# A GNN, token-mixing and routed FFN layer on one core: scattered chunks of four sorted records instead of two, batches of 28 columns instead of 30

## What is computed

```
xn = layernorm(x)
low  = relu(segment_sum(edge_weight    * (xn @ weight_low )[dst], src, N))
high = relu(segment_sum(edge_weight_n2 * (xn @ weight_high)[dst], src, N))
mlp  = relu(xn @ weight_mlp)
att  = softmax(sigmoid([low@a, high@b, mlp@c]) @ att_vec / 3)
gnn  = 3 * (att0*low + att1*high + att2*mlp)
mix  = linear attention of 8 heads over xn (K and V normalised), GELU MLP of 256, plus xn
x    = x + gnn + mix
w    = layernorm(x) @ wr + br
top  = the 3124 rows of largest w
x    = x + layernorm(x) + (top ? (gelu(layernorm(x) @ w1 + b1) @ w2 + b2) * w : 0)
```

## Time and profile before

| what | value |
|---|---|
| timed runs (3) | median 1985.35 us, 1983.74 to 1985.68 |
| profiled execution: span | 2481.7 us |
| mean granted TensorE clock in it | 0.835 |
| busy TensorE, VectorE, ScalarE, POOL | 1719.4, 1229.1, 924.8, 1371.7 us |
| indirect DMAs: scatters, gathers | 448, 852 |
| chain that ended last: TensorE, issue | 51%, 23% |

### The profile page before, as it was taken

How to read it: one execution, slowest core, us unless ns; L and a number is a source line. 1 busy time by engine, 2 the same in 40 slices (tenths; PEclk the granted TensorE clock), 3 DMA queues, 4 the chain that set the end, 5 groups by cost and what they waited for, 6 DMA issues and landing times.

```text
span 2481.7 us, 30518 instructions
## 1 busy us (share of the span) xinstructions
PE 1719.4 (69%) x9109; PEld 1441.9 (58%) x9109; DVE 1229.1 (50%) x3164; ACT 924.8 (37%) x2641; POOL 1371.7 (55%) x1351
## 2 busy tenths in 40 slices
PE   4788884998865347776777677677577677667672
PEld 4566673887754335665665666566466566556562
DVE  8899995888761223432343333333333333333336
ACT  2677873777652112321222222222222222222223
POOL 3277675788776565545555455455455545554600
PEclk9899996999967667888887888788788788788886
DMA  3221211111100422222222222222222222222303
GB/s 90 72 63 54 80 33 30 46 54 46 46 5 5 133 85 72 78 69 75 71 74 71 68 73 75 65 72 75 68 73 75 75 69 71 81 71 68 85 9 104
DMA packets 102212, 162.99 MB, mean 66 GB/s; under 512 B 32190, under 2 KB 72762, under 8 KB 102040
## 3 DMA queue, kind: packets, MB, share of 16 engines
q0 software_dynamic: 55232, 113.59, 16.4%
q1 hardware_dynamic: 46808, 47.29, 6.0%
HBM read 139.76 MB, written 21.04 MB: 65 GB/s over the span
## 4 chain that ended last, share of the span: by engine, by line
PE 51%; issue 23%; DVE 10%; ACT 9%; another core or an unknown queue 5%; DMA 1%; SPq 1%; POOL 0%; DVEq 0%; ACTq 0%; POOLq 0%
PE bank L1528 49%; ACT side L1303 2%; PE bank L1817 1%; ACT base L1303 1%; ACT arena L1303 1%; DVE arena L811 1%; ACT arena L1447 1%; ACT arena L1443 1%; DVE arena L733 1%; ACT side L1519 1%; DVE arena L766 1%; ACT arena L1307 0%; PE bank L1602 0%; DVE arena L781 0%
## 5 line engine op out<-in xcount | busy, mean ns | idle before, releaser
L1528 PE MATMUL bank<-arena 128*128 128x128 f32 (+3 forms) x6320 | 1292.5, 359 | 508.2 <-issue 426.8
L1528 PEld LDWEIGHTS bank<-arena 128*128 128x128 f32 (+1 forms) x6320 | 1094.8, 205 | 683.8 <-issue 500.0
L665 POOL DMA_INDIRECT arena<-xn_rows,arena x852 | 825.5, 969 | 733.8 <-SPq L564 450.0
L648 POOL DMA_INDIRECT sorted_records<-arena x448 | 523.0, 1167 | 256.0 <-issue 139.3
L1167 DVE CUSTOM_DVE_ANT_0 arena<-arena 128x256 f32<-128x256 f32 x98 | 37.8, 423 | 414.9 <-ACT arena L1452 376.1
L1122 DVE TENSOR_TENSOR arena<-arena 128x640 f32<-128x640 bf16 (+1 forms) x204 | 164.2, 805 | 47.6 <-DVE arena L1116 17.7
L1172 DVE SCALAR_TENSOR_TENSOR att_prod<-sg,att_neg 128x9 f32<-128x9 f32 x49 | 8.5, 174 | 334.9 <-issue 300.8
L1490 ACT ACTIVATE arena<-bank 128x256 f32<-128x256 f32 x49 | 18.8, 383 | 355.5 <-remote 262.1
L1116 DVE SCALAR_TENSOR_TENSOR arena<-io,arena 128x320 bf16<-128x320 f32 (+1 forms) x204 | 97.8, 479 | 106.3 <-DVE wall L1209 43.5
L1528 PE MATMUL bank<-arena,base 128*128 128x128 f32 (+3 forms) x766 | 118.4, 287 | 16.7 <-ACT base L1307 8.3
L1438 ACT ACTIVATE arena<-bank,b1f 128x128 f32<-128x128 f32 x392 | 110.3, 372 | 33.5 <-PE bank L1528 28.1
(11 more groups left out here) (312 smaller groups left out, 1889.2 us busy)
## 6 DMA issues: line engine op xcount, KB each, us to landing
arena<-xn_rows,arena POOLq DMA_INDIRECT x852
sorted_records<-arena POOLq DMA_INDIRECT x448
arena<-in_x SPq DMA_DIRECT2D x12, 512.0 KB
xn_rows<-arena SPq DMA_DIRECT2D x12, 512.0 KB
x_plus_xn_rows<-arena SPq DMA_DIRECT2D x12, 512.0 KB
arena<-x_plus_xn_rows SPq DMA_DIRECT2D x12, 512.0 KB
arena<-xn_rows SPq DMA_DIRECT2D x12, 512.0 KB
out<-base SPq DMA_DIRECT2D x4, 1024.0 KB
```

The source lines that it names most:

```text
L648: pool.indirect_dma_start(rec_dram, bass.IndirectOffsetOnAxis(ap=idx[0:PR, par, u:u + 1], axis=0), stage_rec[0:PR, par, u * 8:(u + 1) * 8] ...
L665: pool.indirect_dma_start(gring[:, c % GR, :], None, xn_dram, bass.IndirectOffsetOnAxis(ap=rring[:, c, 3:4].bitcast(I32), axis=0)).then_in ...
L1528: return pe.matmul(out_, lhsT, rhs, start=start, stop=stop, **kw)
```

## The change

A chunk is four records (64 bytes), `REC` = 4. A batch is 28 columns in two groups of 14, so there are 30 batches. A batch is scattered with 8 indirect DMAs and needs 8 small products for the chunks' places. Every bucket's run in a batch is padded to a multiple of four, so the bound on the columns becomes `COLS` = 900, in 8 blocks. All 13 mixing quads stand in slots 14 to 26 (`SPILL` = 0); slots 27 to 29 hold batches 27 to 29, and slot 30 the rest of the last. The first half's quotients are made in a batch's own slot and the second half's at the head of the next slot. The last bucket ends where its records end. The last tile's keys are masked by a memset and a copy of VectorE instead of a selection on POOL. Some small tiles lie elsewhere in memory.

```diff
-HG = 6
-BB = 30
-GS = 10
+HG = 7
+BB = 28
+GS = 14
+REC = 4
@@
-    UNITS = GC // 2
+    UNITS = GC // REC
     STEPS = PR * UNITS
-    CAP = 2 * STEPS
+    CAP = REC * STEPS
@@
-    COLS = 4 * -(-(E + NB * G) // (4 * P))
+    COLS = 4 * -(-(E + (REC - 1) * NB * G) // (4 * P))
@@
-    SPILL = 2
+    SPILL = 0
@@
-        quots = [base[:, spare:T * D].rearrange("p (j q) -> p j q", q=P), side[:, spare:T * D].rearrange("p (j q) -> p j q", q=P),
-                 r1.take([P, GS, P])]
+        quots = [r1.take([P, GS, P]) for _ in range(GROUPS)]
@@ scatter (POOL)
                     pool.indirect_dma_start(
                         rec_dram, bass.IndirectOffsetOnAxis(ap=idx[0:PR, par, u:u + 1], axis=0),
-                        stage_rec[0:PR, par, u * 8:(u + 1) * 8], None).then_inc(S(f"scattered{par}"), 16)
+                        stage_rec[0:PR, par, u * 4 * REC:(u + 1) * 4 * REC], None).then_inc(S(f"scattered{par}"), 16)
@@ end (POOL)
-            pool.wait_ge(S("w_ready"), T)
-            pool.affine_select(out=wkey[:, T - 1:T], in_=wall[:, T - 1:T], compare_op=ALU.is_ge, fill=SENTINEL,
-                               base=TAIL - 1, pattern=[[0, 1]], channel_multiplier=-1).then_inc(S("w_masked"), 1)
@@ sum_hots (VectorE)
-                    dve.tensor_tensor(many[:, :, 0:2], many[:, :, 0:2], many[:, :, 2:4], ALU.add).then_inc(S("many_set"), 1)
+                    dve.tensor_tensor(many[:, :, 0:3], many[:, :, 0:3], many[:, :, 4:7], ALU.add).then_inc(S("many_set"), 1)
...
-                    dve.tensor_tensor(many[:, :, 0], many[:, :, 0], many[:, :, 4], ALU.add).then_inc(S("many_set"), 1)
@@ counts (VectorE)
-            step(dve.tensor_scalar(cnt_b[0:NR, :], cnt_i[0:NR, :], 1, None, ALU.bitwise_and))
-            dve.tensor_tensor(runs[0:NR, :], cnt_i[0:NR, :], cnt_b[0:NR, :], ALU.add).then_inc(S("runs_ready"), 1)
+            step(dve.tensor_scalar(cnt_i[0:NR, :], cnt_i[0:NR, :], REC - 1, None, ALU.add))
+            step(dve.tensor_scalar(cnt_b[0:NR, :], cnt_i[0:NR, :], REC - 1, None, ALU.bitwise_and))
+            dve.tensor_tensor(runs[0:NR, :], cnt_i[0:NR, :], cnt_b[0:NR, :], ALU.subtract).then_inc(S("runs_ready"), 1)
@@ the buckets' table (VectorE)
-            step(dve.memset(pclip[:, NB:NR], float(COLS * P - 1)))
@@ slot (ScalarE)
                 if in_slot(g - 1):
-                    quotients(g - 1, 2, 1 - par)
+                    quotients(g - 1, 1, 1 - par)
...
-                if in_slot(g):
-                    quotients(g, 1, par)
                 if ln is not None:
                     ln_sqrt(ln)
@@ slot (TensorE)
                 if in_slot(g - 1):
                     permute(g - 1, 0, 1 - par)
-                    permute(g - 1, 1, 1 - par)
                 turn(0)
                 if in_slot(g - 1):
-                    permute(g - 1, 2, 1 - par)
+                    permute(g - 1, 1, 1 - par)
                 turn(1)
```

More of the change, by code:

```diff
@@ L283, in build @@
         ptab = lead_take("side", [1, NR], I32)
-        pcol = r1.take([1, NB + 1])
-        starts = r1.take([1, 2, NB])
-        span = r1.take([1, NB])
-        over = r1.take([1, NB])
-        over_sum = r1.take([1, NB])
-        words = r1.take([1, NB])
+        pcol = lead_take("side", [1, NB + 1])
+        starts = lead_take("side", [1, 2, NB])
+        span = lead_take("side", [1, NB])
+        over = lead_take("side", [1, NB])
+        over_sum = lead_take("side", [1, NB])
+        words = lead_take("side", [1, NB])
         far = r1.take([P, 2, NB])
@@ L775, in place @@
                 Q1 = 28
-                with nc.allow_low_precision(reason="whole numbers below 2 ** 13, one of a bucket's and at most nine ties"):
+                with nc.allow_low_precision(reason="whole numbers below 2 ** 13, one of a bucket's and at most thirteen ties"):
                     dve.tensor_tensor(prod[:, :, 0:H], prod[:, :, 0:H], prod[:, :, H:2 * H], ALU.add).then_inc(S("prod_half"), 1)
@@ L1225, in _ @@
             step(dve.memset(const_1_5[:, :], 1.5))
+            step(dve.memset(wkey[:, T - 1:T], SENTINEL))
             def end():
@@ L1416, in _ @@
             quotients(0, 0, 0)
+            ln_sqrt(0)
             quotients(0, 1, 0)
-            ln_sqrt(0)
-            quotients(0, 2, 0)
             stage_records(0, 0)
@@ L1544, in _ @@
             W = H2 * HG
-            PER = 10
+            PER = 8
             for g in range(G):
@@ L1747, in _ @@
             permute(0, 1, 0)
-            permute(0, 2, 0)
             schedule(pe, slot)
```

32 lines of the change are left out of this document (16 added, 16 removed).

## The result

| kernel | median | against the kernel before, same chip |
|---|---|---|
| before | 1983.78 us (5 runs, 1982.85 to 1985.68) | |
| after | 1968.86 us (5 runs, 1965.63 to 1971.53) | 0.992, 95% interval 0.9908 to 0.9932 |

The change makes the kernel 0.8% faster, 15 us, where 23 us slower were forecast. The profiled execution of the kernel after spans 1969.8 us with a mean granted clock of 0.933: no gaps of the kind of the earlier trace rows, so its rows are those of a timed run. That execution spans 1985.4 us at a clock of 0.926, and is free of the gaps too. All rows "of before" from here on are from it.

A forecast was written before the change was run, and what follows sets the result against it. The prediction took POOL as the bound, by scatters in front and then gathers. Front +4, gathers +25.4 and extra turns -6 sum to +23.4, so 1985.35 us becomes 2009 us, range 1964 to 2030.

The forecast's parts named there:

- POOL bounds both parts: Whole kernel before: POOL sets the pace, by scatters from batch 12 on, then by gathers at 1.27 us each.
- Scatters: Front: a batch's scatters cost POOL 24.5 us before and 12 after, so POOL leaves the path.
- A slot with LayerNorm, +0.3 us: Front, LayerNorm slots: the path is ScalarE's quotients and one permute; +0.3 us a slot, +4 over 12, bounds -13 and +13.
- A mixing slot, 22.35 + 1.0 = 23.35 us: Front, mixing slots: own pace 22.35 us; later quotients +1.7, longer permute +1.0, fewer small products -1.7.
- The lower clock: Rival, mixing slots: new idleness drops TensorE's clock; 24.5 us a slot gives 2024 us, 25.5 gives 2037; chance 0.15.
- The slots behind: Front, after the mixing slots: two batch-only slots of 17.5 us, then 28.1 us to the last index and 10.1 of scatters.
- Moving two quads: End of the front: moving mixing quads 11 and 12 ahead of the last batch earns nothing, at most 7 us.
- The 28 other gathers, the eighth block: Buckets: the 28 unneeded gathers run beside the kernel's end, the eighth record block under gathers; 0, block +1.7 without cover.
- Gathers, 20 x 1.27 = +25.4: Buckets: the last bucket needs 872 gathers instead of 852, each 1.27 us on POOL; +25.4 us.
- Extra turns, -6: Last bucket: eight extra turns of 1.9 us go, so it ends 2 us behind the last gather instead of 8; -6 us.
- the slots get faster: Rival, front: TensorE's work is the path, mixing slots take 21.2 us and LayerNorm slots 24.6; 1964 us, chance 0.18.
- the front's 0: Front, from slot 14's copy of ranks to the last scatter: 376.8 us after against 376.6 before, so nothing gained.

The follow-up runs named there:

- e3: The changed kernel with the last two mixing quads behind the batches again; 1970.62 us, 0.9919 of the kernel before.
- e4: The changed kernel with 872 columns instead of 900, leaving out the 28 gathers no bucket needs; 1968.07 us, 0.9898 of the kernel before.
- e2: The changed kernel with chunks of two records again and the last two mixing quads behind the batches; 2008.09 us, 1.0098 of the kernel before.
- e10: The kernel before with the last bucket ending where its records end, and small tiles moved as in the change; 1963.51 us, 0.9882.
- e8: The kernel before, unchanged, profiled again to get a profile without the TensorE gaps; 1987.09 us, span 1985.4 us.
- e5: The kernel before with chunks of four records in its old batches, 868 columns and the last bucket's true end; 1923.69 us, 0.9694.
- e6: The changed kernel with the second half's quotients made in the batch's own slot, in the 13 mixing slots only; 1946.85 us, 0.9815.
- e11: The changed kernel with its 8 small products made twice in each mixing slot; 1974.31 us, 0.9938 of the kernel before.

## Why the prediction was wrong

Its sum was +4 for the front, +25.4 for gathers, -6 for the last bucket. Measured are -20.2, +13.8 and -9.5. By its steps:

- **POOL bounds both parts**, the front from batch 12 on: right. Between 120 and 782 us its 432 scatters waited 46.9 us for places. One wait, ahead of the second batch, is 37.9; the others are seven of 1.0 us and one of 1.8, all ahead of slot 14. Up to there the slots go at VectorE's pace and POOL keeps up with them; behind it POOL has no wait for places at all.
- **Scatters**: 24.5 us for a batch before (24.3 in the mean of the clean profile), about 12 after (10.3 to 13.7 from a batch's first scatter to the end of its last), POOL no longer on the path in front: right.
- **A slot with LayerNorm, +0.3 us**: the first failure of the sum, 10.7 us. It took ScalarE's quotients and a permute for the path. The path is VectorE: before, it works without a pause and the slot takes 24.2 us; with the chunk alone, where half the step mask is gone, 23.9; after, with 22.4 us of work for 23.4, the slot takes 23.5. Up to slot 14 that is -6.7 us where +4 was forecast (-5.3 in the slots with LayerNorm, -1.5 in slot 13). The wait of 2.74 us for the root, from which the prediction took its path, is not there in the clean profile. The prediction had named VectorE's shorter work as a bound of that step, -13 if it counted in full; about half of that came.
- **A mixing slot, 22.35 + 1.0 = 23.35 us**: eight of the twelve full slots take 23.35. The number came out of two errors. The base was 19.95, not 22.35. The rise is +3.4 and +1.8, not +1.0: the small products gave back 0.2 us and not 1.7. By the drawn rows alone, says the prediction of the reading that it turned down, "the slot would cost +2.5"; the mean of the rise is 2.9. The wait of ScalarE by which I overruled the rows was a gap of TensorE like the others: in the clean profile GELU starts 2.8 us after the transposes' drawn end, not 5.25, and waits for nothing (475.35 against 471.92 + 0.60). The Trainium skill's sentence (Perfetto Trace Analysis, Tensor Engine Instruction) that TensorE's ends are estimated is not contradicted by any run, but it was no licence to price these products by something else.
- **The lower clock**: in part. It falls behind the wait of 2.48 us, but comes back in every third slot or so (21.7 us). Eight slots of 23.35, four of these, and the last quad with its single tile (19.2 us) make 293.0 us of 13 slots where 303.6 were forecast. That is the second failure, 10.6 us, of which the single tile alone is 4.1.
- **The slots behind**: two of 17.5 took 32.6 together, the rest 36.6 for 38.2: 4 us. From the copy of slot 14 to the end of the last scatter it is 362.2 us; the forecast was 376.8. For the kernel before it had 376.6, and 375.5 is measured: POOL's pace held it, as the prediction said.
- **Moving two quads**: 0, right (e3). **The 28 other gathers, the eighth block**: 0, right by the rows of e4; its times leave a few us open.
- **Gathers, 20 x 1.27 = +25.4**: twenty cost 25.9 us, but all others came 0.014 us sooner, 12.0 us over 851. The prediction had no such term. Ten of the 12 us are in the gathers themselves, 0.988 us for 1.001, and they are longer where they stand beside VectorE (last section): between 790 and 1870 us 180 of 235 beside VectorE's L1122 take over 1.0 us before, and 138 of 222 beside the same instruction (L1118) after. Why they meet less often is open. The four clean profiles of the old code have 1.301 to 1.307 us between gathers, the nine of the new code 1.292 to 1.295, e2 with its chunks of two among them; so it isn't the chunk, nor the number of columns, and by e10 hardly the tiles.
- **Extra turns, -6**: too small by 3.5. The turns themselves were sized right, 15.2 us. The prediction had the bucket end 8 us behind its last gather with them and 2 without; it is 15.0 and 5.4. Before, TensorE came 4.5 us later than thought and made the last half at the lower clock (2.2 us more). After, the last half starts 3.0 us behind the issue of gather 872, as soon as that is there (0.55 us of waiting for SyncE above), and takes 2.4. That the three new turns hide under gathers is right: POOL never waits for more than 0.3 us there.

The rival "the slots get faster" gave 1964 and had the front at -41. Its time was near, but by luck for a part: its LayerNorm slot (24.6 to be, 23.5 measured) got shorter, by VectorE's work; its mixing slot (21.2; 22.5 measured) did not, it got longer than the 19.95 of before, and what made the stretch shorter was that POOL no longer held it at 24.3 us a batch. **The step that turned the sign** is the front's 0: it was built from slot paces of an execution with 496 us of foreign gaps, and a sum that met the measured time was taken as proof that they had been cleaned out. So the first step that failed is the path of a slot with LayerNorm (over ScalarE, where it is VectorE: -6.7 us for +4), the second the mixing slot's base and clock, and the third a pitch of the gathers that was given no term (-12). With the slots as measured the working gives -20 there, and with the forecast's own +25.4 and -6 it ends at -1: no change. The unforeseen pitch and the last bucket make it -15.6.

## What to carry to other kernels

When a change moves the bound from one engine to the next, the gain is the distance to the next engine's pace (and nothing where another engine bound the stretch already, as VectorE did here in the slots with LayerNorm), so that pace has to be read where the first does not hold it, in an execution that matches the timed one. Where the profiled span is far above the timed runs, get another profile, or a variant's, before pricing anything by it; a reconstruction that meets the total may do so by errors that cancel. And try a change of several parts part by part: here one deleted line was worth 20 us, the larger chunk 72 us in front, and the batches' new shape, which the proof for all inputs asks for, gave 52 of them back.

## What the runs showed that was not expected

- A gather gets longer beside VectorE, and VectorE not beside a gather. After, between 790 and 1870 us, 262 of 835 gathers stand beside no VectorE instruction: they take 0.946 us, none over 1.0. Of the 222 beside L1118 (two operands from SBUF) 138 take over 1.0 us, and the mean of all 222 is 1.075. Of the 72 gathers that start while an L1118 runs, 71 end 0.82 us behind the end of that L1118, whether they started 0.1 us behind its start (1.59 us long) or 0.6 (1.07): they wait for it. Beside L1181 or L1190, short and with one operand, none takes over 1.0 (mean 0.945), nor do the twelve that start beside L1186, one operand of 128x256 and 0.43 us long. VectorE's L1112, always beside a gather, takes 0.48 to 0.49 us each time. A long and a short gather, and the VectorE instructions beside the long one:

```profile
1401.19 1.19 POOL L665 DMA_INDIRECT arena<-xn_rows,arena  x1 [0.30 <-issue]
1402.68 0.95 POOL L665 DMA_INDIRECT arena<-xn_rows,arena  x1 [0.30 <-issue]
...
1401.07 0.48 DVE L1183 SCALAR_TENSOR_TENSOR ybuf<-arena,sg 128x256 f32<-128x256 f32 x1
1401.59 0.48 DVE L1185 SCALAR_TENSOR_TENSOR arena<-side,sg,ybuf 128x256 f32<-128x256 f32 x1
```

  The Trainium skill (GPSIMD Engine Reference, Key points) names operations with two SBUF inputs as those that contend; the rows agree. It is POOL that pays: 0.043 us a gather in the mean, 38 us over 871 of them, on the engine that bounds it. The old trace, whose VectorE stood idle more, showed 0.969 us a gather for 1.001.
- One program left two very different profiles: the earlier trace rows with 454.7 us of TensorE gaps, and e8 without, 1985.4 us for the same code.
- With a single wait of TensorE, of 2.48 us, in a slot, the granted clock is 0.93 over two slots of three and 1.00 over the third (after); in the slot without a wait it is 1.00 (e5), and with one of 1.51 us too (e6).
- A product of 99x2 between others costs TensorE some 0.03 us (e11: 0.2 us a slot for eight).
